# Four attention stages of a fused transformer kernel: value products in bursts of four heads, masks as contraction rows, the maximum as two bf16 rows

## The chip, the cores and the metric

The kernel runs on one core of one Trainium2 chip. The metric is the time of one execution on the device, in microseconds (us); three runs of the kernel before took 5391.18 us in the median (5377.96 to 5403.62). Engines are named as in the profile: PE is TensorE, DVE VectorE, ACT ScalarE, POOL GpSimd, SP SyncE, which issues the DMAs.

## The reference

A model of four layers on x of 16 blocks x 256 tokens x 128 features, fp32. The change touches four of its attention stages; the mixtures of experts, the norms and the linear attention of layer 3 are not touched. The core of each stage is this, per block and head of 8 features:

```python
scores = jnp.einsum('bhqd,bhkd->bhqk', q, k) / scale
scores = jnp.where(jnp.asarray(causal), scores, -jnp.inf)   # a0, a1, a4; a2 has no mask
attn = jax.nn.softmax(scores, axis=-1)
out = jnp.einsum('bhqk,bhkd->bhqd', attn, v)
```

a0 (layer 0) has 16 heads and a gate on q. a1 (layer 1) is a differential attention: 16 pairs of heads, so 32 score matrices, values 16 wide, `attn = softmax(A1) - lam * softmax(A2)`, then an RMS norm per pair. a2 (layer 2) has 16 query heads on one key and value head, biases and no mask. a4 (layer 2) has rotary embeddings on q and k, 16 query heads and 4 key and value heads.

## The kernel before

`attention_phase` is called four times, as a0, a1, a2 and a4. Activations lie as 128 features x tokens. A call works through 16 blocks of 256 tokens in a software pipeline of steps t = -2 to 16. In one step the engines do: the preparation of block t+2 (norm, projection of q, k and v), the row maxima of block t+1, the softmax and value products of block t, and the output projection of block t-1. Each engine's program is its own list, written by the same loop over slots h = 0 to 15 (0 to 31 in a1); constants such as `L_QK`, `L_SPLIT`, `L_NMQ` and `L_MT` say in which slot a piece stands. Engines run their lists in order and wait on semaphores (`after`).

Scores need fp32 accuracy from bf16 products. So q and k are each split into three bf16 parts (`SPL`: hi, mid, lo), and six products of parts are summed by one contraction over 48 rows. The parts are made by ScalarE (hi at L479, mid at L482) and GpSimd (L420, L423), and SyncE moves them into the per-head layout `QH`, `KH` by twelve DMAs a block (L388, L390; 64 KB each, 24 a block in a1; in a2 k has one head and is small). These buffers are three deep. This starts at slot 8 in a0 and a2, 10 in a4, 14 and 18 in a1.

For block t+1, `scores` (L531 to L537) computes q k^T with queries on the partitions, in slots from 2 on (two heads a slot, in a1 about 1.5), and VectorE takes the negated maximum per query (`maxima`, L718, L721). In causal stages only three of the four 128 x 128 tiles are computed, and the mask is added first by a bf16 matmul of an identity with a table, `MASKS` (L531, L548). After the last head, at `L_NMQ` (slot 10, in a1 23), the maxima are transposed (L655) and split into three bf16 rows: ScalarE copies (L487) and casts hi (L490), GpSimd subtracts (L428), ScalarE casts mid (L493), GpSimd subtracts lo (L430). `send_maxima` (L368) issues three DMAs of one row each into rows 66 to 68 of QH. On SyncE's queue they stand behind the ten DMAs of hi and mid parts of block t+2 and ahead of the last two (`a == 2`).

For block t, `scores_t` (L548 to L554) computes the transposed scores, keys on the partitions, with the negated maximum as three more contraction rows against ones (`ONE`). In slot 0 it waits for `m_sent`, the landing of the maxima. ScalarE takes the exponential into `PR` (L507), a ring of four heads; scores alternate between two PSUM banks. `values`, two slots later, multiplies by V with 32 weight columns, whose column VW is one, so that the row sum comes out too (L564, L566); these are fp32 matmuls, each of which the trace shows as two records. Head h writes the 32 partitions of group h % 4. Each set of four heads is copied (`CTS`, L451), transposed back (`turn`, L572) and divided (`turned`, L698, L704). At the start of a stage QH and KH are zeroed by VectorE (`zero_q`, L676) and GpSimd (L398).

## Time and profile before

| | |
|---|---|
| median of three runs | 5391.18 us |
| span of the profiled execution | 5386.6 us (the profiled execution's own time) |
| busy: PE, weight loads, DVE, ACT, POOL | 4688.2, 2569.2, 2625.5, 1708.1, 689.6 us |

The stages, read from the same execution (step 0 begins with the first exponential):

| stage | stretch, us | step 0 begins | step 14 begins | step 15 begins |
|---|---|---|---|---|
| a0 | 27 to 571 | 93.3 | 521.9 | 547.4 |
| a1 | 1458 to 2425 | 1540.4 | 2323.3 | 2372.9 |
| a2 | 3031 to 3556 | 3087.1 | 3501.3 | 3527.0 |
| a4 | 3590 to 4228 | 3654.9 | 4178.6 | 4204.4 |

A row of the timeline or of the groups names the line of the code, the engine, the operation, output<-inputs by tile names, and shapes as partitions x elements; 128\*32 is a matmul with 128 contraction rows and 32 weight columns. A number in brackets is the idle time before it and what ended it. A matmul's length includes the time through the array, and the next one starts before it ends, so the spacing of starts tells what it costs the engine. A row of a window gives the stretch, its length, the busy time and count of PE, PE's weight loads, DVE, ACT and POOL, then the clock, the DMA engines' busy share and GB/s. PEclk, or the clock in a window, is the granted clock: 1.0 is 2.4 GHz, 0.5 is 1.2 GHz.

### The profile page before, as it was taken

The page shows a single profiled execution, that of the slowest core. Times are in us where ns is not written, and L with a number is a line of the kernel's source. Part 1 is how long each engine was busy: PE and PEld are TensorE (multiplying, and loading weights), DVE is VectorE, ACT ScalarE, POOL GpSimd, SP SyncE. Part 2 cuts the span into 40 slices and gives each one's busy share as a digit, 9 for nine tenths or more (in the row PEclk, how much of TensorE's full clock was granted, in tenths as well). Part 3 has the DMA queues.
Part 4 walks back from the last instruction along what each step waited for, and adds up shares of the span by engine and source line. Part 5 has one row for each costly group of instructions (what it writes and reads, how often), then busy time and mean ns, then how long its engine had stood idle before and what let it go on. Part 6 is the DMA issues. An engine that isn't in the chain of part 4 may idle for free. (4 is left out here: it accounts for less than half of the span.)

```text
span 5386.6 us, 77572 instructions
## 1 busy us (share of the span) xinstructions
PE 4688.2 (87%) x21128; PEld 2569.2 (48%) x21128; DVE 2625.5 (49%) x5760; ACT 1708.1 (32%) x3532; POOL 689.6 (13%) x602
## 2 busy tenths in 40 slices
PE   6999679999879999997999799977888799645899
PEld 4555544444446555554444344444555544313544
DVE  3444555555445455545333345443333455798445
ACT  1443232222224444443333244422333322211321
POOL 1111100000022212211000011111111100343100
PEclk7999679999979999997999799978888799555799
DMA  3222100000032223211000000002122000000000
GB/s 54 29 26 24 48 8 0 1 0 0 8 36 35 29 27 36 26 14 38 1 1 0 8 16 14 16 10 25 20 22 23 20 1 0 3 0 4 17 3 16
DMA packets 147700, 88.99 MB, mean 17 GB/s; under 512 B 17933, under 2 KB 144736, under 8 KB 146656
## 3 DMA queue, kind: packets, MB, share of 16 engines
q1 hardware_dynamic: 145695, 82.28, 11.1%
q0 software_dynamic: 576, 1.80, 0.2%
q8 instruction: 127, 2.08, 0.2%
q14 instruction: 150, 1.22, 0.1%
q10 hardware_dynamic: 1152, 1.61, 0.1%
HBM read 26.06 MB, written 2.10 MB: 5 GB/s over the span
## 5 line engine op out<-in xcount | busy, mean ns | idle before, releaser
L548 PE MATMUL bank<-MASKS,IDB 128*128 128x256 bf16 x1024 | 296.3, 289 | 130.8 <-DMA a4QH<-a4M 84.3
L507 ACT ACTIVATE a1PR<-bank 128x384 f32<-128x384 f32 x512 | 248.9, 490 | 410.3 <-PE bank L551 410.0
L718 DVE TENSOR_REDUCE a1NM<-bank 128x3 f32<-128x384 f32 x512 | 269.5, 554 | 200.0 <-PE bank L534 196.2
L531 PE MATMUL bank<-MASKS,IDB 128*128 128x256 bf16 x1024 | 303.8, 297 | 35.3 <-DMA a4QH<-a4SPL 11.8
L1324 DVE TENSOR_TENSOR f1eHS<-f1eSG,bank 128x512 f32<-128x512 f32 x256 | 176.0, 687 | 320.4 <-PE bank L1252 234.5
L1283 ACT ACTIVATE f0eSG<-bank 128x512 f32<-128x512 f32 x256 | 152.9, 597 | 557.9 <-PE bank L1230 557.8
L1319 DVE TENSOR_TENSOR f0eT<-f0eSG,bank 128x512 f32<-128x512 f32 x256 | 176.1, 688 | 311.2 <-PE bank L1233 291.3
L564 PE MATMUL bank<-a1PR,a1VX 128*32 128x256 f32 x1024 | 311.6, 396 | 0.0
L1230 PE MATMUL bank<-f1NT,f1W 128*128 (+1 forms) x576 | 297.7, 599 | 14.6 <-DMA f1eSELB<-in_sel 14.6
L1252 PE MATMUL bank<-f1eHS,f1W 128*128 128x512 f32 x576 | 293.8, 592 | 0.0
L1230 PE MATMUL bank<-f0NT,f0W 128*128 (+1 forms) x512 | 262.9, 595 | 17.4 <-DMA f0eSELB<-in_sel 17.4
L1283 ACT ACTIVATE f1eSG<-bank,f1eFB 128x512 f32<-128x512 f32 x256 | 175.9, 687 | 284.3 <-PE bank L1230 157.1
L1233 PE MATMUL bank<-f0NT,f0W 128*128 (+1 forms) x512 | 262.3, 594 | 0.0
L1252 PE MATMUL bank<-f0eHS,f0W 128*128 128x512 f32 x512 | 261.3, 592 | 0.0
L507 ACT ACTIVATE a4PR<-bank 128x384 f32<-128x384 f32 x256 | 124.8, 488 | 279.4 <-PE bank L551 278.4
L1324 DVE TENSOR_TENSOR f0eHS<-f0eT,bank 128x512 f32<-128x512 f32 x256 | 176.0, 688 | 56.7 <-PE bank L1252 53.4
L548 PEld LDWEIGHTS bank<-MASKS,IDB 128*128 128x128 bf16 x1024 | 104.0, 102 | 196.9 <-DMA a4QH<-a4M 75.4
L507 ACT ACTIVATE a2PR<-bank 128x512 f32<-128x512 f32 x256 | 150.4, 595 | 143.3 <-PE bank L554 142.4
L721 DVE TENSOR_REDUCE a2NMQ<-bank 128x2 f32<-128x512 f32 x256 | 164.7, 685 | 63.7 <-PE bank L537 62.1
L718 DVE TENSOR_REDUCE a4NM<-bank 128x3 f32<-128x384 f32 x256 | 132.2, 553 | 129.0 <-PE bank L534 128.6
L566 PE MATMUL bank<-a1PR,a1VX 128*32 128x128 f32 x1024 | 191.6, 275 | 0.0
L1230 PEld LDWEIGHTS bank<-f1NT,f1W 128*128 128x128 f32 x576 | 109.4, 191 | 155.7 <-issue 154.1
(612 smaller groups left out, 9960.1 us busy)
## 6 DMA issues: line engine op xcount, KB each, us to landing
a1QH<-a1SPL SPq DMA_DIRECT2D x192, 64.0 KB
a1KH<-a1SPL SPq DMA_DIRECT2D x192, 64.0 KB
a0QH<-a0SPL SPq DMA_DIRECT2D x96, 64.0 KB
a0KH<-a0SPL SPq DMA_DIRECT2D x96, 64.0 KB
...
```

Source lines behind the costliest of these rows:

```text
L507: nc.scalar.activation(PR[:, h % 4, :], bank[2 + h % 2][:, 0:NC], ACT.Exp, scale=SCALE)\
L531: pe.matmul(o[:, :].rearrange("p (n x) -> p n x", n=2)[:, :, 0:P], c.IDB[:, :], c.MASKS[:, 0, :, :], start=True, stop=False, skip_group_ch ...
L548: pe.matmul(o[:, :].rearrange("p (n x) -> p n x", n=2)[:, :, 0:P], c.IDB[:, :], c.MASKS[:, 1, :, :], start=True, stop=False, skip_group_ch ...
L564: pe.matmul(o[:, 0:T], v(0), PR[:, h % 4, 0:T], start=True, stop=False)
L566: pe.matmul(rest[0], v(1), rest[1], start=False, stop=True).then_inc(pv_done.sem, 1)
L718: v.tensor_reduce(NM3[:, h, :], bank[h % 2][:, 0:NC].rearrange("p (n k) -> p n k", n=3), AX, ALU.max, negate=True).then_inc(s_used.sem, 1)
L1230: pe.matmul(bank[q][:, :], W1[:, m * P:(m + 1) * P], x, start=True, stop=True).then_inc(g_ready.sem, 1)
L1233: pe.matmul(bank[2 + q][:, :], W3[:, m * P:(m + 1) * P], x, start=True, stop=True).then_inc(u_ready.sem, 1)
L1252: mm = pe.matmul(bank[6 + j][:, :], W2[:, m, :], HS[:, m % 4, :], start=(m == 0), stop=(m == NCH - 1 and CBF is None))
L1283: nc.scalar.activation(dst, bank[q][:, :], fn, bias=FB[:, m:m + 1] if cfg.get("hbias") else 0.0)\
L1319: v.tensor_tensor(T1[:, :], a, bank[2 + q][:, :], ALU.mult).then_inc(t1_ready.sem, 1)
L1324: v.tensor_tensor(HS[:, m % 4, :], a, bank[4 + (j * NBC + kth[m]) % 2][:, :], ALU.mult).then_inc(hs_ready.sem, 1)
```

## The change

Five parts, all in `attention_phase` and its constants:

- **Values.** `values(b, j, u)` now does the four heads of unit u at once, in slots 1, 5, 9, 13, ..., first the first 128 keys of all four column groups, then the second. The last unit of a block falls into slot 1 of the next step. `PR` holds eight heads. Where heads are 8 wide (a0, a2, a4; PK = 2) two units share one set of 32 columns: the weights of one head stand in columns 0 to 15, those of the other, with zeros beside them, accumulate into the rest. So there are two sets to copy, transpose and divide per block, not four. In a1 (PK = 1) there are still eight.
- **Masks.** The mask matmuls go. The mask is now made by contraction rows 48 to 127 of QH and KH, fixed patterns that `mask_rows` makes; tiles off the diagonal use 65 rows only, and `scores` and `scores_t` do three matmuls of 128 columns each.
- **Maximum.** Two bf16 rows in place of three: ScalarE casts hi straight from PSUM, VectorE subtracts it from PSUM to get lo. GpSimd has no part in it. The rows are 48 and 49, which `scores` also reads, so two DMAs of zeros (`ZR`) are sent into them for each block, ahead of the hi parts.
- **Setup.** QH and KH are filled by VectorE copies of the patterns (`fill`) instead of memsets, for each of the three buffers, after two more loads.
- **Order.** The transposes back, the output projection and the waits move with the bursts (`copy_at`, `turn_at`, `L_CTT`).

TensorE's list in a0, from one slot into the next. a0PR holds the exponentials, a0VX the values, a0CTS a set to turn back, a0H and a0WQ, a0WK are the input and weights of the projection. Before:

```order
L548 MATMUL bank<-MASKS,IDB 128x2x128
L550 MATMUL bank<-a0QH,a0KH 128x256
L551 MATMUL bank<-a0QH,a0KH 128x128
L564 MATMUL bank<-a0PR,a0VX 32x256
L566 MATMUL bank<-a0PR,a0VX 32x128
L572 MATMUL bank<-CST,a0CTS 128x128 x2
L531 MATMUL bank<-MASKS,IDB 128x2x128
L533 MATMUL bank<-a0KH,a0QH 128x128
L534 MATMUL bank<-a0KH,a0QH 128x256
```

The same list now, at slot 5:

```order
L569 MATMUL bank<-a0QH,a0KH 128x128
L570 MATMUL bank<-a0QH,a0KH 128x128
L571 MATMUL bank<-a0QH,a0KH 128x128
L592 MATMUL bank<-a0PR,a0VX 32x256 x4
L592 MATMUL bank<-a0PR,a0VX 32x128 x4
L630 MATMUL bank<-a0H,a0WQ 128x256
L631 MATMUL bank<-a0H,a0WK 128x256
L551 MATMUL bank<-a0KH,a0QH 128x128
L552 MATMUL bank<-a0KH,a0QH 128x128
L553 MATMUL bank<-a0KH,a0QH 128x128
```

The pair of value products, which stood in every slot, now stands in every fourth, for four heads; no matmul reads MASKS.

SyncE's list in a0, one step: the DMAs of a0SPL (parts of q and k of the next but one block) and a0M (maxima of the next). Before:

```order
L388 DMA a0QH<-a0SPL 8x16x256 [waits hi_ready]
L390 DMA a0KH<-a0SPL 8x16x256
...
L390 DMA a0KH<-a0SPL 8x16x256 [waits mid_ready]
L388 DMA a0QH<-a0SPL 8x16x256 x2
L390 DMA a0KH<-a0SPL 8x16x256
L368 DMA a0QH<-a0M 1x16x256 [waits mlo_ready]
L368 DMA a0QH<-a0M 1x16x256 x2
L390 DMA a0KH<-a0SPL 8x16x256 [waits lo_ready]
L388 DMA a0QH<-a0SPL 8x16x256
```

And now:

```order
L419 DMA a0QH<-a0ZR 1x16x256 [waits hi_ready,st_ready]
L419 DMA a0QH<-a0ZR 1x16x256
L423 DMA a0QH<-a0SPL 8x16x256
L425 DMA a0KH<-a0SPL 8x16x256
...
L425 DMA a0KH<-a0SPL 8x16x256 [waits mid_ready]
L423 DMA a0QH<-a0SPL 8x16x256 x2
L425 DMA a0KH<-a0SPL 8x16x256
L402 DMA a0QH<-a0M 1x16x256 [waits mlo_ready]
L402 DMA a0QH<-a0M 1x16x256
L425 DMA a0KH<-a0SPL 8x16x256 [waits lo_ready]
L423 DMA a0QH<-a0SPL 8x16x256
```

Two one-row DMAs came in ahead of the parts, one of the maxima went; the place of the maxima behind ten DMAs of parts stays.

The diff, cut to its core:

```diff
-MROW = 66
-KROWS = MROW + 3
+MAX0 = ROWS
+FREE = 65
+def mask_rows():
+    q, k = np.zeros((96, 2, P), np.float32), np.zeros((96, 2, P), np.float32)
+    i = np.arange(P)
+    up, lo = np.array([2.0 ** 36, 2.0 ** -17, 0.0]), np.array([0.0, -2.0 ** -16, -2.0 ** 37])
+    k[MAX0 - 32:MAX0 - 30] = 1.0
+    for tile, row in ((0, 50 - 32), (1, 57 - 32)):
+        for n in range(4):
+            q[row + n, tile], k[row + n, tile] = i // 27 == n, -2.0 ** 64 * (i // 27 > n)
...
+    PK = 2 if VW == 8 else 1
+    NU = NH // 4
+    NS = NU // PK
+    KROWS = P if causal else FREE
+    head = lambda p: p if PK == 1 else p // 8 * 8 + 2 * (p % 4) + p // 4 % 2
...
-        L_LAST, L_COMBINE = 1, 2
-        L_CTT, L_OUT, L_TMP = (9, 10, 10) if diff else (3, 4, 5)
+        burst_at = lambda h: ((h - 5) // 4 % NU, 0 if h >= 5 else -1) if h % 4 == 1 else None
+        copy_at = {(4 * PK * (s + 1) + 2) % NH: (s, (4 * PK * (s + 1) + 2) // NH) for s in range(NS)}
+        turn_at = {4 * PK * (s + 1) + 4: s for s in range(NS)}
+        L_LAST = 4 * PK * NS + 4 - NH
+        L_COMBINE = L_LAST + 2
+        L_CTT = L_COMBINE + 4 if diff else L_LAST + 2
...
             def send_maxima(t, m):
                 after(sp, mlo_ready, t + 1)
-                for a in range(3):
-                    sp.dma_start(QH[MROW + a:MROW + a + 1, (m + 1) % 3, :, :], M3[:, a, :]).then_inc(m_sent.sem, 16)
+                for a in range(2):
+                    sp.dma_start(QH[MAX0 + a:MAX0 + a + 1, (m + 1) % 3, :, :], M2[:, a, :]).then_inc(m_sent.sem, 16)
...
+                            for z in range(2 if r == a == 0 else 0):
+                                sp.dma_start(QH[MAX0 + z:MAX0 + z + 1, j, :, :], ZR[:, :]).then_inc(parts_sent[0].sem, 16)
...
-                    pe.matmul(o[:, :].rearrange("p (n x) -> p n x", n=2)[:, :, 0:P], c.IDB[:, :], c.MASKS[:, 1, :, :],
-                              start=True, stop=False, skip_group_check=True)
-                    pe.matmul(o[:, 0:T], k(0), q, start=False, stop=False, skip_group_check=True)
-                    mm = pe.matmul(o[:, T:3 * P], k(1), q[:, P:T], start=False, stop=True, skip_group_check=True)
+                    pe.matmul(o[:, 0:P], k(0), q(0), start=True, stop=True)
+                    pe.matmul(o[:, P:2 * P], k(0, FREE), q(1, FREE), start=True, stop=True)
+                    mm = pe.matmul(o[:, 2 * P:3 * P], k(1), q(1), start=True, stop=True)
...
-                pe.matmul(o[:, 0:T], v(0), PR[:, h % 4, 0:T], start=True, stop=False)
-                rest = (o[:, P:T], PR[:, h % 4, T:3 * P]) if causal else (o[:, 0:T], PR[:, h % 4, T:2 * T])
-                pe.matmul(rest[0], v(1), rest[1], start=False, stop=True).then_inc(pv_done.sem, 1)
+                for n in range(2):
+                    for g in range(4):
+                        p = 4 * u + g
+                        v = vslot(head(p))
+                        x = v % PK * 2
+                        w = VX[:, j, n * (SV // PK) + v // PK, x:x + 2, :].rearrange("p q x -> p (q x)")
+                        o = bank[4 + s % 2][32 * g:32 * g + 32, P if n and causal else 0:T]
+                        rhs = PR[:, p % 8, n * T:min(NC, n * T + T)]
+                        mm = pe.matmul(o, w, rhs, start=(a == 0 and n == 0), stop=(a == PK - 1 and n == 1), skip_group_check=True)
+                mm.then_inc(pv_done.sem, 1)
...
-                        nc.scalar.copy(MF[:, :], bank[7][0:NH, 0:T]).then_inc(mf_ready.sem, 1)
+                        nc.scalar.copy(M2[:, 0, :], bank[7][0:NH, 0:T]).then_inc(mhi_ready.sem, 1)
...
+                        if h == L_MSPLIT:
+                            after(v, mhi_ready, b)
+                            v.tensor_tensor(M2[:, 1, :], bank[7][0:NH, 0:T], M2[:, 0, :], ALU.subtract).then_inc(mlo_ready.sem, 1)
...
-            zero_q = lambda j: v.memset(QH[:, j, :, :].rearrange("p h t -> p (h t)").bitcast(F32), 0.0).then_inc(q_zeroed, 1)
+            def fill(j):
+                if j == 0:
+                    v.wait_ge(rows_in, 32)
+                for rows in (slice(32, 64), slice(64, KROWS)):
+                    for dst, src, n in ((QH, QC, NH), (KH, KC, HK)):
+                        v.tensor_copy(dst[rows, j, :, :], src[rows, :].unsqueeze(1).to_broadcast([rows.stop - rows.start, n, T])).then_inc(rows_ready, 1)
```

## Rows read from the trace of the kernel before

**Rows 1.** a0, a1, a2, a4, first exponential of step 0 to that of step 14: stretch, length, busy (count), clock, DMA.

```profile
93.30:521.90 428.60, 399.53 (x2676) 247.53 (x2675) 179.34 (x485) 175.18 (x406) 60.61 (x70) 0.94 0.26 27
1540.40:2323.30 782.90, 757.88 (x5141) 463.18 (x5140) 398.88 (x1110) 325.71 (x726) 163.58 (x111) 0.98 0.28 31
3087.10:3501.30 414.20, 405.43 (x2228) 200.03 (x2226) 205.91 (x471) 193.57 (x392) 60.64 (x70) 0.98 0.06 15
3654.90:4178.60 523.70, 430.43 (x2711) 269.02 (x2710) 182.20 (x500) 170.17 (x404) 80.45 (x98) 0.86 0.21 22
```

**Rows 2.** TensorE timeline in a0, one head: start, length, instruction, count.

```profile
350.92 0.22 PE L533 MATMUL bank<-a0KH,a0QH 66*128 66x128 bf16 x1
350.98 0.27 PE L534 MATMUL bank<-a0KH,a0QH 66*128 66x256 bf16 x1
...
351.59 0.22 PE L551 MATMUL bank<-a0QH,a0KH 69*128 69x128 bf16 x1
351.74 0.62 PE L564 MATMUL bank<-a0PR,a0VX 128*32 128x256 f32 x2
352.19 0.38 PE L566 MATMUL bank<-a0PR,a0VX 128*32 128x128 f32 x2
352.50 0.44 PE L572 MATMUL bank<-CST,a0CTS 128*128 128x128 f32 x2
```

**Rows 3.** TensorE timeline at a step's end in a1: two heads of value products back to back.

```profile
1929.17 0.63 PE L564 MATMUL bank<-a1PR,a1VX 128*32 128x256 f32 x4
1929.63 0.39 PE L566 MATMUL bank<-a1PR,a1VX 128*32 128x128 f32 x4
1929.95 0.70 PE L583 MATMUL bank<-XT,CST 128*128 x2
```

**Rows 4.** TensorE timeline: first score product of a step, a0 and a4; brackets: the wait.

```profile
367.42 0.28 PE L548 MATMUL bank<-MASKS,IDB 128*128 128x256 bf16 x1 [1.57 <-DMA a0QH<-a0M]
...
3915.22 0.40 PE L548 MATMUL bank<-MASKS,IDB 128*128 128x256 bf16 x1 [5.79 <-DMA a4QH<-a4M]
```

**Rows 5.** ScalarE timeline in a0: the cast that ends part T.

```profile
352.33 0.61 ACT L479 CAST a0SPL<-a0QKF 128x512 bf16<-128x512 f32 x1
```

**Rows 6.** SyncE timeline, DMA issues in a0 and a1.

```profile
352.96 0.61 SPq L388 DMA_DIRECT2D a0QH<-a0SPL  x1
353.62 0.61 SPq L390 DMA_DIRECT2D a0KH<-a0SPL  x1
...
360.67 1.83 SPq L368 DMA_DIRECT2D a0QH<-a0M  x3
...
1921.47 1.84 SPq L368 DMA_DIRECT2D a1QH<-a1M  x3
```

**Rows 7.** Windows of part T in a0, a4, a1, a2 (columns as rows 1).

```profile
337.40:352.30 14.90, 14.90 (x101) 9.99 (x102) 8.96 (x22) 4.82 (x11) 0.70 (x1) 0.89 0.00 0
3878.40:3900.00 21.60, 21.60 (x137) 14.42 (x137) 11.97 (x30) 5.97 (x14) 2.16 (x3) 0.84 0.00 0
1877.40:1899.90 22.50, 22.32 (x161) 14.68 (x162) 14.71 (x40) 8.69 (x20) 6.12 (x2) 1.00 0.01 2
3298.80:3311.90 13.10, 13.00 (x75) 7.09 (x76) 9.69 (x21) 5.61 (x12) 0.70 (x1) 1.00 0.00 0
```

**Rows 8.** Windows in a4: TensorE idle before M lands, and the stretch after it.

```profile
3872.70:3878.40 5.70, 0.00 (x1) 0.01 (x1) 0.00 (x0) 0.69 (x2) 0.00 (x0) 0.71 0.52 48
3878.40:3885.30 6.90, 6.90 (x34) 4.64 (x34) 2.86 (x9) 1.47 (x3) 0.71 (x1) 0.50 0.00 0
```

**Rows 9.** Answers on the tiles a1M, then a2M: their DMAs from issue to landing.

```profile
DMA to landing us min/median/max: 2.1/2.7/10.0
...
DMA to landing us min/median/max: 1.8/1.8/2.4
```

**Rows 10.** VectorE: a memset of QH (timeline, a0) and the maxima (page, a1).

```profile
47.44 1.76 DVE L676 MEMSET a0QH<- 69x2048 f32 x1 [0.37 <-issue]
...
L718 DVE TENSOR_REDUCE a1NM<-bank 128x3 f32<-128x384 f32 x512 | 269.5, 554 | 200.0 <-PE bank L534 196.2
```

More of the change, by code:

```diff
@@ L448, in copy_set @@
             def copy_set(b, s):
[L449 removed]
+                after(act, pv_done, b, PK * (s + 1))
                 after(act, t_ready, b, s - 1)
@@ L809, in step @@
                             v.tensor_tensor(DST[:, tok(b)], DST[:, tok(b)], TMP[:, :], ALU.add).then_inc(x_updated.sem, 1)
-                    if has(0, t) and h - 1 in turn_at:
-                        turned(t, m, turn_at[h - 1])
-                if has(0, t) and NH - 1 in turn_at:
-                    turned(t, m, turn_at[NH - 1])
+                    for s, back in late(h - 1, turn_at):
+                        if has(-back, t):
+                            turned(t - back, (m - back) % 3, s)
                 if isinstance(t, int) and t < 0:
-                    zero_q(t + 3)
+                    fill(t + 3)
             steps(v, step)
```

245 lines of the change are left out of this document (115 added, 130 removed).

## The prediction

> **What bounds the kernel now.** First the busy time per stage: in the four attention loops TensorE is busy 93%, 97%, 98% and 82% of the time [rows 1]; a0, a1 and a2 look bound by it, a4 by something else. Divided by 14 steps, the four stretches give 30.6 us a step in a0, 55.9 in a1, 29.6 in a2 and 37.4 in a4.
>
> Next the TensorE timeline of one head, where starts count, not durations, since matmuls overlap [rows 2]: a 128-column bf16 matmul takes 0.06 us of the engine (L533 to L534), so one of 256 about 0.11. The value products take 0.15 (L551 to L564, of which 0.06 is L551's own columns), 0.45, and 0.31 up to L572, together about 0.76 us beyond L551, of which two gaps of 0.1 us lie where the engine goes from 128-column to 32-column weights and back. A causal head has 640 columns of mask and scores twice (256 + 128 + 256), 0.28 us each, and so costs 0.28 + 0.28 + about 0.85 with its gaps = 1.4 us.
>
> Then what TensorE waits for. In a0 it ends each step with a wait for the row maxima (M), which a DMA writes into QH: 1.57 us at 367.42 in a0, 5.79 us at 3915.22 in a4 [rows 4]. So a step is a loop of two parts. Part T runs from the landing of M to the cast that produces the high part of q and k of two blocks on; part L from that cast to the next landing, since SyncE issues ten 64 KB transfers first and M behind them. In a0, T is 14.9 (337.4 to 352.3 [rows 7]) and L is 352.33 to 367.42 = 15.1; in a4, 21.6 and 15.2 [rows 4, 7], where each window of rows 7 ends at a cast. L holds no TensorE work: 8.3 us from the cast to M's first DMA at 360.67, filled by the ten issues, then 6.8 us until all three rows have landed behind the backlog [rows 4, 5, 6]. M lands before TensorE needs it in a1 and a2. A faster TensorE shortens only T.
>
> **The change, part by part.** *Value products.* One burst of four heads in four 32-column groups replaces four separate pairs. Where before already runs two heads back to back, all eight records of both heads take 1929.17 to 1929.95 = 0.78 us [rows 3], what one head takes alone: the groups run side by side. I price a burst of four at 0.81 us, bounds 0.78 and 3.1 (four heads in a row at 0.76 each, nothing overlapped); the nearest row says 0.81. That is 0.2 us a head instead of 0.76.
> The Trainium skill (TensorE: Matmul & The Clock Gate, Part 3, "Packing small matmuls") reports 2.38x for three column tiles instead of nearly 3x; the trace's pair shows nearly 2x. By the page's efficiency a burst would be an estimated 0.95 us, which adds under 0.5 us to a step.
>
> *Masks.* The mask matmul goes; three of 128 columns remain, 3 x 0.06 = 0.18 instead of 0.28 us, twice a head. Bounds 0.17 and 0.30 (if weight loads of 0.1 us each, as their records last, did not overlap); the L533 to L534 spacing says 0.06. That 128 contraction rows cost what 66 do I assume; the bound covers it. In all a causal head falls from 1.4 to 0.56 us, the rest of a step (projections, transposes) stays near 4 to 9 us, so TensorE needs about 14 us a step in a0 and a4, 27 in a1.
>
> *Part T.* VectorE takes over. It does not get less work before the cast: 8.96 us in a0, 14.71 in a1, 9.69 in a2, 11.97 in a4 [rows 7], and it starts two slots after the landing and waits at each burst. With TensorE at full clock T is that work plus the late start and one stall of 0.6 to 0.8 us (a burst's length) per burst: 8.96 + 1.5 = 10.5 in a0, 14.71 + 3.3 = 18 in a1, 9.69 + 1.8 = 11.5 in a2, 11.97 + 2.5 = 14.5 in a4, where a GpSimd addition comes last. But the clock will fall: TensorE is then idle 6 to 9 us before each landing. a4 shows the price today: after 5.7 us without a matmul the clock is at 0.5 (1.2 GHz) for the next 6.9 us [rows 8]. Those 6.9 us do 3.5 us of TensorE's work in T (some 9 us in a 16-head stage, 13.5 in a1, at full clock). As VectorE would have waited for part of it anyway, I add 2 us, less in a2, where the idle time is shortest: T = 12.5 in a0, 20 in a1, 12.8 in a2, 17 in a4.
> The Trainium skill (same page, Part 1, "HAM oscillation") has a rule that speaks against the change: an engine that idles between bursts is throttled and restarts cold in every round. Rows 8 show that, and the sum above goes by their 6.9 us.
>
> *Part L.* The hi/mid/lo chain of the maxima over ScalarE and GpSimd (third row included) becomes one ScalarE cast and one VectorE subtraction from PSUM. That chain is not what ends last in L: SyncE's ten transfers are. Two one-row zero transfers are now issued ahead of them, 2 x 0.61 us by M's own issue rate (1.83 for 3 [rows 6]); one M row fewer gives back 0.6 to 0.9. Net +0.5: L = 15.6 in a0 and a4, bounds 14.5 and 17. In a1, 22 transfers precede M; cast at 1899.9, M issued at 1921.47, its third row 1.2 later, landed by the median 2.7 after that, 25.5 in all [rows 6, 7, 9]; other rows took up to 10.0 us, so 27, bounds 25 and 30. In a2 K is one head and small; M's issue follows twelve others at 0.66 [rows 6]: 0.6 + 7.9 + 0.4, and lands 2.4 later (1.8 after the second row's issue [rows 9]): 11.4.
>
> Step after: a0 12.5 + 15.6 = 28.1 (-2.5), a1 47 plus 1 for the loop's branch (-8), a2 24.2 (-5.4), a4 32.6 (-4.8). Sum -20.7 a step, x14 = -290 us. The last two steps of each stage have no such transfers ahead, and there most of the TensorE saving counts: 49.6 + 52 us in a1, about 49 in each other stage, by the stage table; 20 us saved in a1 and 13 in each of the three others, about -60.
>
> *Setup.* DMA of patterns and VectorE copies (L701) replace memsets of QH and KH. A memset of 2048 fp32 took 1.76 us; each of four copies in a fill of a 16-head stage moves 4096 bf16, the same bytes: 1.8 us, nearest to that row; bounds 0.9 (half of it) and 5.6 (1.37 ns an element, as the 384-element maxima, 269.5 us / 512, run) [rows 10]. The first fill stands ahead of everything on VectorE and waits for two more loads: about +8 us in a0 and a4, +14 in a1, +3 in a2; later fills lie under transfers that TensorE waits for anyway. Sum +30, bounds 15 and 110.
> The Trainium skill (VectorE: DVE Perf Modes, "Mode 4x_2P") would give a bf16 copy four elements a cycle, an estimated 1.1 us; the sum would fall by about 12 us.
>
> Total: -290 - 60 + 30 = -320 on the profiled execution's own 5386.6: 5067. The median of the runs lies 4.6 above that, so **5071 us**.
>
> **Rivals.** *A. More.* L shortens or overlaps (M lands soon after its issue as in a2), or the clock holds, so T is VectorE's floor: steps of 25, 42, 22.5 and 28.5, together -35.5 x 14 = -497, with ends and setup 4864. For: M's first issue needs only 8.5 us. Against: in a0 and a4 TensorE's wait ended with M's landing in every step.
> *B. Less.* Bursts overlap only in pairs (1.55 us): two bursts in T of the 16-head stages, four in a1, partly at half clock, +9.5 a step over all stages: 5071 + 133, about 5205. For: only a pair is seen in the trace.
> *C. Not what it says.* Four groups don't overlap at all (3.1 us a burst): T grows by 2.3 for each burst in it, 4.6 and in a1 9.2: steps of 32.7, 57, 28.8 and 37.2, +2.2 a step; the ends give half: 5420, at the edge of what can be told from no change.
> *D. Slower.* TensorE, idle in every step, never returns to 2.4 GHz within a stage. Its work in T doubles: T = 17.6, 27, 19, 21.5; steps 33.2, 54, 30.4, 37.1, together +1.2 x 14 = +17, no gain at the ends, setup +25: 5433 us. It decides as soon as half-clock stretches last beyond the cast; 6.9 us in a4, with TensorE fully busy at half clock, speaks against.
>
> **How the numbers follow.** Forecast 0.65; A 0.11; B 0.13; C 0.04; D 0.07. The forecast's own range, by the bounds of L, the copies and the burst, is 4980 to 5170; A and B widen the 8-in-10 range to 4940 to 5250. Half a per cent is what a measurement of this kernel can tell: faster 0.89, same 0.04, slower 0.07.
>
> **What would show it.** Right: TensorE's wait for M grows to 6 to 9 us a step in a0 and a4 and appears in a1; its clock is at 0.5 in every step; L stays near 15.6; four value groups start within 0.05 us of each other; TensorE's busy time falls by 600 us or more while the time falls by 320. Wrong: M lands under 12 us after the cast in a0 (A), burst records spaced 0.2 us (B, C), or T above 17 in a0 (D).

## The result, and the profile after

| | before | after |
|---|---|---|
| median, us (four runs each) | 5397.4 | 5226.3 (5204.5 to 5241.7) |
| span of the profiled execution | 5386.6 | 5202.7 |
| step in a0, a1, a2, a4 (loop of 14 / 14) | 30.6, 55.9, 29.6, 37.4 | 29.9, 52.8, 26.8, 34.0 |
| mean clock in the four loops | 0.94, 0.98, 0.98, 0.86 | 0.75, 0.82, 0.73, 0.69 |

The ratio after/before is 0.968 (95% interval 0.965 to 0.971): 3.2% faster. I had forecast 5071 us, 5.9% faster, so the likeliest value is 155 us too low. The 8-in-10 range, 4940 to 5250, holds the result; the forecast's own range, 4980 to 5170, does not.

The page of the kernel after: span, TensorE's busy time, and the clock that was granted in 40 slices.

```profile
span 5202.7 us, 74298 instructions
PE 3966.3 (76%) x20936; PEld 2258.1 (43%) x20936; DVE 2662.3 (51%) x5663; ACT 1611.0 (31%) x3308; POOL 593.5 (11%) x462
PEclk9777679999968888877999867766677798556699
```

TensorE is busy 722 us less than before (4688.2), the time falls by 184 us between the two profiled executions. The same four loops as in [rows 1], same columns:

```profile
101.20:520.30 419.10, 270.61 (x2611) 189.64 (x2608) 172.82 (x443) 151.26 (x348) 42.12 (x42) 0.75 0.26 28
1514.20:2253.70 739.50, 492.82 (x5124) 355.50 (x5123) 414.63 (x1120) 310.56 (x697) 145.04 (x83) 0.82 0.29 32
3005.10:3380.20 375.10, 332.13 (x2162) 173.27 (x2160) 199.42 (x429) 170.61 (x334) 44.65 (x42) 0.73 0.07 17
3534.80:4011.40 476.60, 275.53 (x2642) 199.84 (x2639) 174.25 (x458) 146.42 (x347) 62.52 (x70) 0.69 0.23 24
```

Two things are to be seen. PE's share of a0's stretch fell from 93% to 65%, that of a4 from 82% to 58%: it waits. And the clock, before near 1 but for a4, is between 0.69 and 0.82.

The wait is the one of [rows 4]. TensorE's timeline, first score product of a step in a0 and in a1:

```profile
335.95 0.29 PE L569 MATMUL bank<-a0QH,a0KH 128*128 128x128 bf16 x1 [9.16 <-DMA a0QH<-a0M]
1988.59 0.29 PE L569 MATMUL bank<-a1QH,a1KH 128*128 128x128 bf16 x1 [5.52 <-DMA a1QH<-a1M]
```

In all, the profile has TensorE wait 135 us for a0's M, 96 for a1's, 161 for a4's: 8.5 us a step in a0 (16 of them), 10 in a4. The first exponential of a step stands 0.6 or 0.7 us behind M's landing in every step of a0 and a4. So there the step is T + L, as forecast. The windows below are part T of a0 (335.90 to the cast at 349.50), the beginning of that T, L of a0, T of a1 up to its first cast, T of a2, a stretch that begins 1 us before that T, then T and L of a4:

```profile
335.90:349.50 13.60, 13.24 (x110) 9.67 (x110) 7.32 (x19) 4.71 (x11) 0.70 (x1) 0.63 0.00 0
335.90:346.10 10.20, 10.04 (x84) 7.45 (x84) 5.33 (x14) 3.58 (x8) 0.70 (x1) 0.50 0.00 0
349.50:365.90 16.40, 6.44 (x79) 4.07 (x78) 5.07 (x14) 6.17 (x15) 2.31 (x2) 0.81 0.47 50
1988.50:2013.90 25.40, 20.79 (x180) 15.55 (x184) 15.31 (x40) 9.11 (x20) 6.12 (x2) 0.68 0.01 2
3268.90:3285.70 16.80, 16.06 (x90) 8.69 (x90) 8.91 (x19) 5.73 (x12) 0.70 (x1) 0.62 0.02 4
3267.90:3281.50 13.60, 12.31 (x70) 6.82 (x70) 6.40 (x14) 4.34 (x8) 0.70 (x1) 0.50 0.02 6
3873.80:3891.50 17.70, 15.87 (x151) 11.87 (x151) 11.32 (x28) 5.75 (x14) 2.16 (x3) 0.76 0.00 0
3891.50:3907.90 16.40, 3.59 (x39) 2.42 (x39) 1.22 (x5) 4.79 (x12) 2.31 (x2) 0.64 0.47 50
```

The rows that answer to [rows 7] have a clock of 0.62 to 0.76 where those of before had 0.84 to 1.00, and TensorE is the busy engine of T in every stage (in a0 13.24 of 13.6 us, VectorE 7.32), where the forecast had VectorE take over. After 9.2 us of waiting the clock stays at 0.50 for the next 10.2 us, although TensorE is busy for 10.04 of them. In a2, behind a wait of 3.1 us, it is at 0.50 for the 12.4 us that follow M's landing at 3269.1. [Rows 8] had led me to expect 6.9.

The value burst (TensorE's timeline in a1, at full clock) answers to [rows 2, 3]: all 16 records of four heads, then the next product.

```profile
2001.50 0.86 PE L592 MATMUL bank<-a1PR,a1VX 128*32 128x256 f32 x16
2002.29 0.23 PE L551 MATMUL bank<-a1KH,a1QH 128*128 128x128 bf16 x1
2002.36 0.22 PE L552 MATMUL bank<-a1KH,a1QH 65*128 65x128 bf16 x1
```

2001.50 to 2002.29 is 0.79 us; forecast 0.81. The four groups' first records start at 2001.50, .51, .52 and .52. The score products after it stand 0.06 to 0.07 us apart, as forecast.

SyncE's issues in a0 behind the cast of 349.53, to set beside [rows 6]:

```profile
350.17 1.20 SPq L419 DMA_DIRECT2D a0QH<-a0ZR  x2
351.41 0.68 SPq L423 DMA_DIRECT2D a0QH<-a0SPL  x1
...
358.22 1.21 SPq L402 DMA_DIRECT2D a0QH<-a0M  x2
```

Means over the steps of blocks 1 to 12, from each landing of M and each start of a cast in the trace (in a1 to the first of its two casts, as in the prediction):

| | T forecast | T after | L forecast | L after | step forecast | step after |
|---|---|---|---|---|---|---|
| a0 | 12.5 | 13.4 | 15.6 | 16.7 | 28.1 | 30.1 |
| a1 | 20 | 25.3 | 27 | 28.1 | 48 | 53.4 |
| a2 | 12.8 | 14.9 | 11.4 | 11.7 | 24.2 | 26.5 |
| a4 | 17 | 17.8 | 15.6 | 16.4 | 32.6 | 34.2 |

The loop is the forecast one, and every term of it is longer than I made it. The experiments ask why.

### The profile page after: what moved, and what is told of

It reads as the page before. It is cut to its first block and busy times, and to the rows that moved or that the text cites. A ratio compares the mean times of both kernels' runs of the same rounds, so it can differ in the third digit from the quotient of the medians.

```text
span 5202.7 us, 74298 instructions
## 1 busy us (share of the span) xinstructions
PE 3966.3 (76%) x20936; PEld 2258.1 (43%) x20936; DVE 2662.3 (51%) x5663; ACT 1611.0 (31%) x3308; POOL 593.5 (11%) x462
## 5 line engine op out<-in xcount | busy, mean ns | idle before, releaser
L1254 PE MATMUL bank<-f1NT,f1W 128*128 (+1 forms) x576 | 297.4, 598 | 15.1 <-DMA f1eSELB<-in_sel 15.1
L1348 DVE TENSOR_TENSOR f0eHS<-f0eT,bank 128x512 f32<-128x512 f32 x256 | 176.0, 688 | 54.6 <-PE bank L1276 49.6
L569 PE MATMUL bank<-a1QH,a1KH 128*128 128x128 bf16 x512 | 123.3, 245 | 103.7 <-DMA a1QH<-a1M 95.8
L527 ACT ACTIVATE a0PR<-bank 128x384 f32<-128x384 f32 x256 | 121.1, 488 | 227.2 <-PE bank L571 225.6
L569 PE MATMUL bank<-a4QH,a4KH 128*128 128x128 bf16 x256 | 65.7, 258 | 161.9 <-DMA a4QH<-a4M 161.1
L551 PE MATMUL bank<-a1KH,a1QH 128*128 128x128 bf16 x512 | 126.2, 248 | 70.9 <-DVE a1NM L744 64.7
L569 PE MATMUL bank<-a0QH,a0KH 128*128 128x128 bf16 x256 | 63.2, 250 | 136.2 <-DMA a0QH<-a0M 135.4
## 6 DMA issues: line engine op xcount, KB each, us to landing
f0W<-in_w SPq DMA_DIRECT2D x3, 2048.0 KB, 12.8
```

The source lines that it names most:

```text
L527: nc.scalar.activation(PR[:, h % 8, :], bank[2 + h % 2][:, 0:NC], ACT.Exp, scale=SCALE)\
L551: pe.matmul(o[:, 0:P], q(0), k(0), start=True, stop=True)
L569: pe.matmul(o[:, 0:P], k(0), q(0), start=True, stop=True)
L1254: pe.matmul(bank[q][:, :], W1[:, m * P:(m + 1) * P], x, start=True, stop=True).then_inc(g_ready.sem, 1)
L1348: v.tensor_tensor(HS[:, m % 4, :], a, bank[4 + (j * NBC + kth[m]) % 2][:, :], ALU.mult).then_inc(hs_ready.sem, 1)
```

## The experiments

Each kernel is after with one edit, unless said otherwise, timed beside the kernel before on the same chip. The table has the median, the ratio to before with its 95% interval, and the steps (the loop of 14 divided by 14) of the profiled execution.

| | us | ratio to before | a0 | a1 | a2 | a4 |
|---|---|---|---|---|---|---|
| before | 5388 to 5397 | 1 | 30.6 | 55.9 | 29.6 | 37.4 |
| after | 5226 | 0.968 (0.965, 0.971) | 29.9 | 52.8 | 26.8 | 34.0 |
| e1 zero rows last | 5172 | 0.961 (0.959, 0.963) | 28.0 | 51.8 | 27.2 | 33.5 |
| e2 M from ScalarE | 5105 | 0.946 (0.942, 0.950) | 27.2 | 50.7 | 25.9 | 32.2 |
| e3 fill the wait, 64 rows | 5411 | 1.004 (1.002, 1.006) | 32.6 | 54.6 | 26.9 | 42.0 |
| e4 mask cost, 64 rows | 5747 | 1.064 (1.059, 1.069) | 38.5 | 65.0 | 27.4 | 44.7 |
| e5 fill the wait, 128 rows | 5226 | 0.971 (0.967, 0.974) | 29.5 | 52.7 | 26.6 | 33.1 |
| e6 mask cost, 128 rows | 5312 | 0.987 (0.984, 0.990) | 31.1 | 54.7 | 26.8 | 36.2 |
| e7 K's parts from ScalarE | 5141 | 0.956 (0.952, 0.960) | 28.8 | 50.8 | 25.6 | 33.9 |
| e8 a1's transposes later | 5125 | 0.953 (0.948, 0.958) | 29.5 | 46.6 | 27.0 | 34.5 |
| e9 all products 128 rows | 5183 | 0.963 (0.959, 0.966) | 29.2 | 52.9 | 25.6 | 34.0 |
| e10 combination | 4975 | 0.921 (0.916, 0.927) | 26.4 | 45.0 | 26.4 | 31.0 |
| e11 combination | 5094 | 0.944 (0.941, 0.947) | 29.4 | 47.1 | 26.7 | 33.9 |
| e12 combination | 5029 | 0.933 (0.929, 0.936) | 27.4 | 45.8 | 26.6 | 31.1 |

### What stands ahead of M on the queue

**e1.** The zero rows go last (for a1: last of its first set).

```diff
-                            for z in range(2 if r == a == 0 else 0):
-                                sp.dma_start(QH[MAX0 + z:MAX0 + z + 1, j, :, :], ZR[:, :]).then_inc(parts_sent[0].sem, 16)
                             for n, pair in enumerate(PAIRS):
...
+                            for z in range(2 if r == 0 and a == 2 else 0):
+                                sp.dma_start(QH[MAX0 + z:MAX0 + z + 1, j, :, :], ZR[:, :]).then_inc(parts_sent[0].sem, 16)
```

> After, with one edit: the two transfers of zero rows into QH are issued behind the last parts of the first (in the 16-head stages the only) set of heads, so that there they stand behind M's two transfers instead of ahead of all. Theory (the step is a loop, T + L, and the zero rows stand at the head of L): the zero rows hold the first 64 KB transfer back by 1.2 us, and L falls by as much in a0 (16.7 to 15.5), a4 (16.4 to 15.2) and a2 (11.7 to 10.5), not in a1, where they stay ahead of M: 3 x 1.2 x 15 = 54 us, 5172 us. Rival (M lands when the bytes of the ten transfers have drained, and the zero rows cost nothing beside them): L unchanged, within 10 us of 5226.

5172, the theory's time to the microsecond, but not by its split, so that the exact match is luck. L is 15.1 in a0 (-1.6), 15.6 in a4 (-0.8), 10.4 in a2 (-1.3), which is what the theory said in kind. But in a2 T grew by 2.0 in that execution and the step became longer (27.3 from 26.5), in a0 T fell by 0.4, where TensorE waits less, and a1, where the theory had nothing, gained 1 us a step. One step of a0: the cast, SyncE's first issue and M's, and the end of TensorE's wait for M.

```profile
330.44 0.61 ACT L504 CAST a0SPL<-a0QKF 128x512 bf16<-128x512 f32 x1
331.07 0.68 SPq L421 DMA_DIRECT2D a0QH<-a0SPL  x1
...
337.87 1.21 SPq L402 DMA_DIRECT2D a0QH<-a0M  x2
...
345.61 0.29 PE L569 MATMUL bank<-a0QH,a0KH 128*128 128x128 bf16 x1 [7.24 <-DMA a0QH<-a0M]
```

The first 64 KB transfer is issued 0.63 us behind the cast; in after it was 1.88 (349.53 to 351.41). M lands 15.1 behind the cast. The term that I had netted out ("one M row fewer gives back 0.6 to 0.9") did not come: in a0 L is 1.2 us longer than in the kernel before (16.7 for 15.5), as long as the issue of the zero rows. The zero rows stand at the head of the backlog, where they move all of it.

**e2.** M's two transfers on ScalarE's queue.

```diff
+                    if has(1, t) and h == L_MSPLIT + 1:
+                        after(act, mhi_ready, t + 1)
+                        after(act, mlo_ready, t + 1)
+                        for a in range(2):
+                            act.dma_start(QH[MAX0 + a:MAX0 + a + 1, (m + 1) % 3, :, :], M2[:, a, :]).then_inc(m_sent.sem, 16)
```

(and `send_maxima` leaves SyncE.)

> After, with M's two transfers issued by ScalarE's own queue, one slot after the maxima are split, instead of by SyncE behind ten (a1: 22) others. Theory (L is M's place in SyncE's queue): the wait for M goes. What is late next is the parts themselves, which scores of the next block need in slot 2 instead of slot 0: the loop loses about 2.5 us of T and 0.5 of L. Steps of about 26.5 in a0 (from 30.1), 49 in a1 (from 53.4), 23.5 in a2 (from 26.5), 31.3 in a4 (from 34.2): -13.9 x 14 = -195, 5031 us. Rival 1 (the transfers already drain at the rate of the engines, M's packets wait for them from any queue): M still lands 16 us after the cast, 5226. Rival 2 (issuing and waiting on ScalarE holds up its exponentials): slower than 5240.

5105: the theory holds in kind, with 121 of the 195 us. TensorE's waits in the loop of a0:

```profile
PE bank L565 <- DMA a0QH<-a0M: 41.8, 13, 4.3
PE bank L547 <- DMA a0QH<-a0SPL: 19.8, 12, 3.1
```

M is waited for 3.2 us a time instead of 8.5, and the parts, as expected, in their turn (19.8 us in a0, 70 in a4). But M does not land at once from its own queue: in a0 its second transfer is issued 6.0 us behind the cast, and the step begins 11 to 14 us behind it, after a wait that ends with M. That is the part of rival 1 that holds: something is shared behind the queues.

**e7.** K's six transfers per set on ScalarE's queue.

```diff
-                                if pair[1] == a:
-                                    sp.dma_start(KH[rows, j, 16 * r:16 * r + min(HK, 16), :], SPL[0:KR, r, a, 1, :]).then_inc(parts_sent[r].sem, 16)
...
                                 nc.scalar.copy(SPL[:, r, 0, :, :], QKF[:, :, :]).then_inc(hi_ready.sem, 1)
+                                after(act, st_ready, b - 3)
+                                after(act, hi_ready, b, r + 1)
+                                send_keys(b, (m + 2) % 3, r, 0)
```

> After, with the six transfers of K's parts (per set of heads) issued by ScalarE's queue, those of Q, the zero rows and M by SyncE's as now. Theory (L is the drain of one queue, 65 KB a us of 64 KB transfers): two queues drain side by side, and M stands behind five parts instead of ten: L about 11 in a0 and a4 (from 16.7 and 16.4), 8 in a2, 16 in a1 (from 22.2), steps 25, 29, 23, 47: -19.5 x 14 = -273, 4953 us. Rival (the 16 DMA engines are the limit, whichever queue feeds them): L less by at most 1 us, 5226 to 5190. Second rival (ScalarE's issues, 0.6 us each, delay its exponentials in T): slower.

5141, and the rate decides between them. Transfers in flight in a0 (last two columns: busy share of the DMA engines, GB/s), after with one queue:

```profile
353.00:365.00 12.00, 3.56 (x41) 2.45 (x41) 1.87 (x7) 3.83 (x10) 0.35 (x1) 0.78 0.63 64
```

and this kernel with two:

```profile
338.00:349.00 11.00, 7.16 (x60) 4.31 (x52) 2.99 (x9) 5.41 (x13) 1.16 (x1) 0.64 0.64 66
```

64 GB/s and 66 GB/s: the second queue adds nothing to the rate, so the first rival is right that the queues share one rate, and the forecast of L about 11 is wrong. That the DMA engines themselves are the limit is not shown: their busy share is 0.63 and 0.64 in these rows. L falls by 1.1 in a0, 0.3 in a4, 1.5 in a2. The gain in all (86 us) is more than that rival allowed; the loop of a1, with 24 transfers to issue at 0.66 us each on one queue, gives 28 of it, a2 16, a0 16, a4 2.

What fills L in the 16-head stages is this drain, not the number of issues, and not only of what stands ahead of M. In the first row 12 us at 64 GB/s are 768 thousand bytes, and M lands behind it, at 365.9; the ten transfers ahead of M are 655 thousand bytes, all twelve of the step 786 thousand. In every step of a0 and a4 M landed 0.2 to 1.0 us behind the last packet of all twelve. So M, though issued ahead of the last two, waited for them as well: about 12 us of transfers plus the start.

### What the clock costs, and what it goes by

**e3.** Matmuls that nobody reads ahead of the wait for M.

```diff
                 if p == 0:
+                    if not (isinstance(b, int) and b < 1):
+                        for _ in range({"a0": 70, "a1": 45, "a2": 24, "a4": 80}[cfg["name"]]):
+                            pe.matmul(bank[2][:, 0:T], KC[64:P, 0:P], KC[64:P, :], start=True, stop=True)
                     after(pe, m_sent, b)
```

> After, with matmuls of 256 columns that nobody reads ahead of TensorE's wait for M: 70 in a0, 45 in a1, 24 in a2, 80 in a4 (0.107 us each at full clock: 7.5, 4.8, 2.6, 8.6 us, within the wait that is there now). Theory (T is long because TensorE idles, comes back at 1.2 GHz for 10 us or more, and is the busy engine of T): granted clock 1.0 in T; T 10.5 instead of 13.4 in a0, 27 instead of 31.3 in a1, 12.5 instead of 14.9 in a2, 15.5 instead of 17.8 in a4; -11.9 x 14 = -167, 5060 us. Rival 1 (VectorE bounds T, the clock is beside the point): 5226 within 20. Rival 2 (the added matmuls outlast the wait or draw the clock down): slower.

5411: rival 2, slower than after by 185 us and than before by 0.4%. Three rows of a0: the added matmuls of a step in which TensorE had been idle for 6.24 and 2.64 us shortly before, the stretch after them, and the added matmuls of the next step:

```profile
339.80:354.20 14.40, 14.40 (x68) 9.75 (x66) 0.15 (x1) 0.42 (x1) 0.00 (x0) 0.50 0.00 0
354.20:362.20 8.00, 7.89 (x63) 6.23 (x63) 3.60 (x10) 2.48 (x6) 0.70 (x1) 0.50 0.01 2
374.80:382.60 7.80, 7.77 (x71) 6.45 (x70) 0.42 (x1) 0.69 (x2) 0.00 (x0) 1.00 0.66 58
```

In the first, TensorE works without a gap for 14.40 us and the clock is at 0.50 all the time and for the 8 us after. So an idle engine is not the only one that gets 1.2 GHz. In the third, the same 70 matmuls take 7.8 us at 1.00. Of the fifteen such stretches in a0, twelve are like the third and three like the first; in a4 fourteen of fifteen take 17.2 us at 0.50. So these matmuls kept a clock that was high, and did not bring back one that had fallen. Nor was it safe behind them: after eight of the twelve in a0 it fell again within 8 us. The added matmuls contract 64 rows (partitions 64 to 127).

**e5.** The same with all 128 rows (`KC[:, 0:P], KC[:, :]`, rows 0 to 31 of KC set to zero).

> As the run with added matmuls ahead of the wait for M (70, 45, 24, 80), but each contracts 128 rows instead of 64; their time per column is the same. There, TensorE worked through the added matmuls at 1.2 GHz (0.213 us each, 14.5 us in a0) and the clock did not rise. Theory (what the clock goes by is not whether TensorE has work but how much of the array it uses): with 128 rows it stays at 2.4 GHz through the wait, the added matmuls fit into it, T falls to 10.5 in a0, 27 in a1, 12.5 in a2, 15.5 in a4: 5060 us. Rival (rows don't matter, the clock goes by something else): as there, 5411 us.

5226, 185 us less than e3 for the same instructions and columns. Here are the added matmuls in a step of a0, and T behind them:

```profile
355.00:362.80 7.80, 7.80 (x71) 6.76 (x70) 0.42 (x1) 0.74 (x2) 0.00 (x0) 1.00 0.66 59
364.50:374.90 10.40, 9.42 (x110) 6.66 (x110) 7.26 (x19) 4.74 (x12) 0.70 (x1) 1.00 0.01 2
```

The clock is 1.00 in both, and T is 10.40 us (10.2 to 10.9 in the steps of a0 without the loop's branch): the number that the prediction had worked out for full clock (10.5) and the 10.5 expected here. VectorE is busy for 7.26 us of it and TensorE for 9.42. Yet the kernel is no faster than after, 166 us above the theory. One reason is in the timeline of TensorE; every third step of a0 begins as the first rows here, the others as the last two:

```profile
322.99 0.79 PE L613 MATMUL bank<-XT,CST 128*128 x1 [6.74 <-issue]
326.45 0.79 PE L613 MATMUL bank<-XT,CST 128*128 x1 [2.67 <-issue]
327.04 9.88 PE L567 MATMUL bank<-a0KC 128*128 128x256 bf16 x70
...
354.99 7.82 PE L567 MATMUL bank<-a0KC 128*128 128x256 bf16 x70
364.52 0.23 PE L574 MATMUL bank<-a0QH,a0KH 128*128 128x128 bf16 x1 [1.71 <-DMA a0QH<-a0M]
```

In one step of three, where the loop's branch is, TensorE waits 6.74 and 2.67 us for its own instructions ("issue"), the added matmuls begin late and outlast M's landing: 38 us for that step, 27 for the others. In the loop of a0 in after no wait ends by "issue"; whether the stall lies under the wait for M there is not shown. The other reason is that T did not fall in a1 (25.3) and hardly in a2 (14.6), where 4 and 2.4 us less were expected; in a4 it is near 15.2 in the steps without the branch.

What the rows are worth shows where like is set beside like. With the clock high at their start, the added matmuls took 7.8 us at 1.00 with 64 rows and with 128. Behind the idle time of the branch it was 15.11 us at 0.50 in e3 and 9.88 us at 0.78 here, in a4 17.2 us against 8.9 to 11.7; and behind them the clock was at 1.00 for 8 us after every stretch of a0. So with 128 rows the clock came back while the matmuls ran, with 64 it did not. Of the 185 us a4 gives 125 and a0 43. The contents of the added rows differ too, since rows 0 to 31 are zeros.

**e4, e6.** The cost of the old mask product put back, as a matmul of 256 columns ahead of each causal group, with 64 and with 128 rows.

```diff
                 if causal:
+                    pe.matmul(o[:, 0:T], KC[64:P, 0:P], KC[64:P, :], start=True, stop=True)
```

> After, with the TensorE cost of the old mask product put back: one 256-column bf16 matmul ahead of every causal score group, overwritten by the group's first two products, 2 per head and block, in a0, a1 and a4. Theory (TensorE's time counts only in T, where it runs at half clock): in a 16-head stage 21 of the 32 lie in T, 0.21 us each, +4 us a step in a0, +3 in a4, +4 in a1 (42 of 64, partly under waits): +154, 5380 us. Rival (TensorE's saved time is all idle time now): within 20 of 5226. Second rival (all of it counts, as before): 2 x 16 x 0.11 = 3.5, 3.5 and 7 us a step plus half clock, over 5450.

> As the run with a 256-column matmul ahead of every causal score group, but with 128 contraction rows, as the old mask product had, instead of 64. There the time rose to 5747, by three times what I expected, with 74% of the loop of a0 at 1.2 GHz. Theory (use of the array holds the clock, as above): the same time on TensorE but at full clock for most of T: at most 3.5 us a step in a0 and a4, 7 in a1, less what the clock gives back: 5270 us. Rival (clock independent of the rows): 5747.

5747 and 5312. The loop of a0 with 64 rows:

```profile
98.20:636.50 538.30, 465.03 (x3057) 242.02 (x3056) 183.80 (x443) 152.97 (x348) 42.07 (x42) 0.64 0.20 22
```

and with 128:

```profile
97.80:533.00 435.20, 304.89 (x3059) 228.73 (x3057) 175.93 (x443) 151.00 (x348) 42.09 (x42) 0.78 0.25 27
```

Clock 0.64 against 0.78, T 22.3 against 14.5 us, for the same columns. The expectation of e4 (5380) failed by 367 us, and e6, at 5312 for 5270, shows what was wrong with it: not the count of matmuls, but the clock that they ran at. e6 less after, 86 us, is what the removed mask products are worth in this loop: 16-head stages gain 1.2 and 2.2 us a step, a1 1.9, though 3.5 and 7 us of TensorE's time go.

**e9.** The score products of 65 rows contract 128 (`FREE` to `KROWS`; in a2 the added rows are filled as in the other stages).

```diff
-                    pe.matmul(o[:, P:2 * P], k(0, FREE), q(1, FREE), start=True, stop=True)
+                    pe.matmul(o[:, P:2 * P], k(0), q(1), start=True, stop=True)
```

> After, with the score products that contract 65 rows (the off-diagonal third of each causal group; in a2 all of them) contracting 128. In a2 the added rows of Q are zeros; in the causal stages they lay a mask on the off-diagonal tile too, so that the output is another one. Columns, instructions and transfers stay as they are, so that TensorE's work takes the same time at the same clock. Theory (rows in use decide what clock is granted, and the maxima's loop pays for it in T): less of the loops at 1.2 GHz, most in a2 (now 50%, where it should fall below 20%), T 12.5 instead of 14.9 there, 12.6 in a0 (from 13.4), 1 us less in a1, 0.8 in a4: -5 x 14 = -70, 5156 us. Rival (the rows of real products don't matter, only those of the matmuls added in the wait): 5226 within 15.

5183, 43 us less (the intervals of the two ratios overlap by 0.001), where the theory had 70 and the rival less than 15. It is clearest in a2, where every score product changes:

```profile
3008.10:3367.10 359.00, 278.68 (x2163) 151.11 (x2160) 197.46 (x429) 170.17 (x333) 45.13 (x42) 0.89 0.07 18
```

0.89 instead of 0.73, 25.6 us a step instead of 26.8, with the same instructions; T is 14.0, where 12.5 was expected, from 14.9. The added rows of Q hold zeros there, so the clock did not need values in them. In the causal stages, where one product of three changes, the clock rises by 0.02 to 0.04; a0 gains 0.7 us a step, a1 and a4 nothing. The output of this kernel is another one than the model's, by its edit, so it serves for the time alone.

### a1

In a1 T was 5.3 us longer than forecast. There VectorE waits for GpSimd's power (`CR`). Timeline of the two in after:

```profile
1999.52 5.43 POOL L461 TENSOR_TENSOR a1CR<-a1CM,HALF 128x32 f32<-128x32 f32 x1 [6.12 <-DVE a1CM L819]
2004.98 0.69 DVE L823 TENSOR_TENSOR a1CX<-a1CX,a1CR 128x512 f32<-128x512 f32 x1 [2.94 <-POOL a1CR L461]
```

and in before, where VectorE comes to the result 3.6 us after it is there:

```profile
1880.06 5.43 POOL L433 TENSOR_TENSOR a1CR<-a1CM,HALF 128x32 f32<-128x32 f32 x1 [0.71 <-DVE a1CM L794]
...
1889.11 0.68 DVE L798 TENSOR_TENSOR a1CX<-a1CX,a1CR 128x512 f32<-128x512 f32 x1
```

GpSimd needs 5.43 us in both. Before, seven slots lay between `L_COMBINE` (2) and `L_CTT` (9); now four (6 and 10), and slots are shorter. Waits in the loop of a1, after:

```profile
PE bank L672 <- DVE a1CX L735: 48.2, 13, 3.7
DVE a1CX L823 <- POOL a1CR L461: 37.6, 13, 3.0
```

**e8.** `L_CTT` (with `L_OUT`, `L_TMP`) four slots later; two waits of TensorE move with it and are not shown.

```diff
-        L_CTT = L_COMBINE + 4 if diff else L_LAST + 2
+        L_CTT = L_COMBINE + 8 if diff else L_LAST + 2
```

> After, with a1's transposes of CX (and what follows them: CXN on VectorE, output product, residual) four slots later, 14 instead of 10. GpSimd's power over 32 elements (5.43 us) would then be behind other work. Theory (in a1 VectorE waits 2.9 us and TensorE 3.7 us a step for it, both in T): T of a1 28 instead of 31.3, -3.3 x 14 = -46, 5180 us. Rival (TensorE waits elsewhere instead, as the transposes now stand between two turns on the same bank): within 10 of 5226.

5125. VectorE's wait for GpSimd (L823) is no longer among the waits; TensorE's wait is halved:

```profile
PE bank L672 <- DVE a1CX L735: 23.3, 13, 1.9
```

T of a1, to the first cast, is 19.0 us (forecast 20), the step 46.9 as a mean over the same blocks (forecast 48). The gain is twice what was expected: -102 us, not -46, more than the wait that goes (2.9 us of VectorE's, 1.8 of TensorE's a step). The clock is part of it: in after it falls again in every step of a1, behind this wait (0.50 from 2004.9 to 2011.7 in the step shown above, M having landed at 1988.5), and in e8 it does not fall there; the mean clock of a1's loop rose from 0.82 to 0.86. How the gain divides between the two is not settled.

### Combinations

**e10.** M and the zero rows on ScalarE's queue, transposes later. **e11.** K's parts on ScalarE's queue, zero rows last, transposes later. **e12.** Zero rows last, transposes later, and 42, 20, 8 and 56 added matmuls of 128 rows. Their edits are those above.

> After, with three edits: M's transfers and those of the zero rows on ScalarE's queue, and a1's transposes four slots later. If the gains are additive: -121 (M from ScalarE) - 102 (transposes later) - 20 (zero rows no longer ahead of the parts): 4985 us. Rival: a1's part of the first (-38) is not there once a1's T is shorter, 5020.

> After, with three edits: K's parts on ScalarE's queue, the zero rows issued last by SyncE, a1's transposes four slots later. Additive: -86 - 102 - 54 = 4984 us. Rival: the zero rows' 54 is in part the same time as the 86 (both shorten what stands ahead of M): 5010.

> After, with zero rows issued last, a1's transposes four slots later, and 128-row matmuls ahead of the wait for M, fewer than in the two runs with 70 of them: 42 in a0, 20 in a1, 8 in a2, 56 in a4, so that they end before M lands. The first two alone should give 5226 - 54 - 102 = 5070. Theory (the clock that the wait costs is worth 1 to 2 us a step): 5010. Rival (T no longer hangs on the clock, or the idle rest of the wait lets it fall all the same): 5070.

e10 is the fastest, 4975 us, 7.9% below before; additive, within 10 us of what was expected. Its loop of a0:

```profile
93.00:463.00 370.00, 270.39 (x2610) 187.95 (x2609) 172.91 (x443) 149.81 (x347) 42.15 (x42) 0.80 0.29 32
```

e11 misses by 110 us and is slower than its rival too: in a0 and a4 both edits shorten what stands ahead of M, and the rate of the transfers stays; a0's step is 29.4, longer than with either edit alone (28.0, 28.8), and its L 16.4 (15.1 and 15.7 alone). Why it is longer and not the same is open. e12 at 5029 lies 41 below the sum of its first two edits, which by itself says little, since e11 missed its sum by 110; T speaks for the clock, 12.3 in a0 and 16.0 in a4, from 13.0 and 18.0 in e1. Its loops of a0, a1 and a4:

```profile
95.00:478.70 383.70, 315.53 (x3199) 231.73 (x3196) 172.66 (x443) 151.36 (x347) 42.12 (x42) 0.89 0.29 30
1489.50:2130.00 640.50, 495.44 (x5406) 354.86 (x5404) 412.01 (x1120) 306.35 (x697) 148.45 (x83) 0.90 0.33 38
3392.30:3827.50 435.20, 350.41 (x3425) 259.54 (x3423) 173.51 (x458) 146.30 (x347) 62.56 (x70) 0.86 0.25 27
```

The clock is 0.89, 0.90 and 0.86 (in after 0.75, 0.82, 0.69). In a0 and a4 the added matmuls end before M lands, also in the step with the branch: the first exponential stands 0.6 us behind the landing, in e5 3.3 and 2.3 us in the mean.

## Why the prediction was right, and where it promised too much

**Right.** That the step is a loop T + L, and that TensorE stands idle in it until M lands, for 6 to 9 us in a0 (8.5; a4 slightly above, 10) and also in a1; the value burst (0.79 for 0.81); the score products (0.06 each); TensorE's busy time (-722, forecast at least -600). The rivals B, C (bursts that overlap only in part) fall with the burst's rows, D (slower) with the clock, which comes back in every step of a0 and a4, and with T of a0 (13.4, where D had 17.6), A with L and T. The ends of the stages: from step 14 to the stage's last instruction it is 32.9, 91.4, 46.8 and 32.1 us after, against 49.0, 104.0, 51.7 and 49.1: -51 for -60. The setup up to step 0 grew by 16 us in sum, forecast 30 (of the 184 us of the profiled executions, 10 lie outside the four stages); the copies take 1.2 us and more in a 16-head stage, 2.5 in a1 (forecast 1.8 and twice that):

```profile
L701 DVE COPY a1KH<-a1KC 32x8192 bf16<-32x8192 bf16 x3 | 7.8, 2595 | 0.0
L701 DVE COPY a0QH<-a0QC 32x4096 bf16<-32x4096 bf16 x3 | 3.7, 1217 | 8.0 <-DMA a0KC<-in_krows 7.9
```

The Trainium skill (VectorE: DVE Perf Modes, "Mode 4x_2P"), from which an estimated 1.1 us was worked out, is close to the shortest of them, 1.2 us.

**Right in the number, not in the reason.** "VectorE takes over" did not come. In T of a0, a2 and a4 TensorE is busy for 13.24 of 13.6, 16.06 of 16.8 and 15.87 of 17.7 us, VectorE for 7.32, 8.91 and 11.32; and even at full clock, in e5, it is 9.42 against 7.26 of 10.4. So the 10.5 us of a0 at full clock, summed from VectorE's 8.96 and a late start, was met by another engine's work: luck. The range held by luck too: only its widening to 5250, made for A and B, reaches 5226, and B's bursts in pairs are not what happened.

**Too much: the sum of the loops.** -290 was forecast, -139 came (the four loops' lengths, 2149.4 before and 2010.3 after). The working that failed, in order of its size:

1. *T in a1: 25.3 for 20*, 5 us x 14 = 74 us. The prediction built it on VectorE's 14.71 us of work plus a late start and stalls for the bursts, and overlooked that VectorE's list waits for GpSimd's 5.43 us, started four slots before its use instead of seven. That cover was gone once TensorE no longer filled the slots. e8, which puts eight slots between the two, gives T = 19.0; part of that is the second fall of the clock, which goes with the wait.
2. *The clock: "those 6.9 us"*: T is 0.9, 2.1 and 0.8 us longer in a0, a2 and a4, 53 us. The price was taken from one step of the kernel before, [rows 8]. In after the stretch at 1.2 GHz goes on for 6.8 to 10.9 us behind M's landing in a0 and 6.6 to 10.8 in a4. In a0 the clock alone accounts for it: without its fall T is 10.4 (e5). In a2, where the least was expected, the clock falls also in steps in which TensorE waits 1.3 us for M or less (at 0.50 from 3247.4 to 3254.2, TensorE busy throughout); e9, with a mean clock of 0.89 there, gives back 0.9 of the 2.1 us, and the rest is open.
3. *L: 16.7 for 15.6 in a0, 16.4 in a4, 28.1 for 27 in a1*, 0.3 in a2: 46 us. The zero rows were priced by SyncE's issue time and netted against the M row that goes. e1 shows that they count in full (L falls by 1.6, 0.8 and 1.3 us in a0, a4 and a2 without them at the head), since the whole backlog starts later. That M lands behind the ten transfers ahead of it was the forecast's picture; it lands behind all twelve, which the L read from the kernel before already contained.

The three sum to 173 us, for 151 that were missing; the steps' means leave out the first and last of the loop and the "plus 1 for the loop's branch" counted in the forecast.

Why the clock is lower than in the kernel before at the same or a smaller busy share is in part open. e4 against e6, e3 against e5, and e9 show that the same columns with fewer contraction rows can go with a lower clock, and the change took the mask matmuls, 128 rows, out of the causal stages. a2 never had them, and there the score products contracted 66 and 69 rows before and 65 now. A score product and the first value product of before, in the whole of a2, and the value products of after, in its loop:

```profile
L553 PE MATMUL bank<-a2QH,a2KH 69*128 69x256 bf16 x256 | 70.9, 280 | 0.0
L564 PE MATMUL bank<-a2PR,a2VX 128*32 128x256 f32 x512 | 151.1, 396 | 0.0
L592 PE MATMUL bank<-a2PR,a2VX 128*32 128x256 f32 x880 | 87.3, 534 | 0.0
```

So the rows of the score products alone did not take a2's clock from 0.98 to 0.73. What changed beside them is the share of the value products, which contract 128 rows: in the loop of a2 they were 260 of TensorE's 405 busy us before (L564 and L566) and are 87 of 332 now. Whether that is the cause, or the waits are, no run tests; e9 shows that 128 rows in the score products bring back 0.16 of the 0.25.

The Trainium skill (TensorE: Matmul & The Clock Gate, Part 1, "HAM oscillation") had been weighed as a rule against this change, and in a0 and a4 the trace agrees with it: TensorE idles 8.5 and 10 us each step and restarts at 1.2 GHz. The Trainium skill (same page, Part 1, "What's actually happening") has the clock go by how busy the engine has been; e3, where it has no gap for 14.4 us (17.2 in a4) and stays at 1.2 GHz, does not agree with that alone, and the measurement decides.
